# First attention of a two-layer transformer kernel: GpSimd makes the layernorm's mean and variance of batches 0 to 6 by trees of additions, in place of VectorE's statistics

## The reference, cut to what matters

```python
def _layernorm(x, axis=-1, eps=1e-05):
    m = jnp.mean(x, axis=axis, keepdims=True)
    v = jnp.var(x, axis=axis, keepdims=True)
    return (x - m) / jnp.sqrt(v + eps)

x = L0_attn_x                                        # [8, 512, 128]
x = _layernorm(x + _L0_attn_ref(x, L0_attn_W_qkv), axis=-1)   # this layernorm is changed
x = _layernorm(x + _L0_ffn_ref(x, ...), axis=-1)     # mixture of experts
x = _layernorm(x + _L1_attn_ref(x, ...), axis=-1)    # attention with sigmoid weights
x = _layernorm(x + _L1_ffn_ref(x, ...), axis=-1)

def _L0_attn_ref(x, W_qkv):                          # 16 heads of 8 columns
    q, k, v = jnp.split(x @ W_qkv, 3, axis=-1)
    scores = jnp.einsum('bhnd,bhmd->bhnm', heads(q), heads(k)) / jnp.sqrt(128.0)
    attn = jax.nn.softmax(scores, axis=-1)
    return jnp.einsum('bhnm,bhmd->bhnd', attn, heads(v))   # back to [8, 512, 128]
```

## Time and profile before

| | |
|---|---|
| median of three runs | 1043.27 us (1043.18 to 1043.75) |
| profiled execution, first to last instruction | 1041.4 us |
| mean granted TensorE clock in it | 0.996 of full speed |
| repeat of one batch in the first attention | 44.15 us |
| VectorE busy, share of the span | 834.0 us, 80% |
| GpSimd busy, share of the span | 475.6 us, 46% |

### The profile page before, as it was taken

The page is one execution under the profiler, slowest core; times in us unless marked ns, Lnnn a source line. Parts: engine busy times, 40 slices in busy tenths (PEclk is TensorE's granted clock), DMA queues, the critical chain, the costliest instruction groups (busy, mean ns, idle before and its releaser), DMA issues. The chain is left out here.

```text
span 1041.4 us, 20120 instructions
## 1 busy us (share of the span) xinstructions
PE 995.5 (96%) x5835; PEld 475.4 (46%) x5835; DVE 834.0 (80%) x1874; ACT 729.9 (70%) x939; POOL 475.6 (46%) x483
## 2 busy tenths in 40 slices
PE   8899999999999999999999999999999999999996
PEld 3222222222222235888888887873332333222485
DVE  6889999999999977787888789897666666643677
ACT  2078777787777786555555555568898888899754
POOL 0332514325053725676777677576442244220275
PEclk9999999999999999999999999999999999999998
DMA  6553222131321003344324323443512331230011
GB/s 198 153 186 119 76 76 89 44 117 46 96 78 52 3 2 101 102 128 145 101 91 156 121 90 117 137 137 102 172 65 61 121 119 63 60 122 1 1 31 52
DMA packets 73981, 97.04 MB, mean 93 GB/s; under 512 B 12669, under 2 KB 42237, under 8 KB 73533
## 3 DMA queue, kind: packets, MB, share of 16 engines
q1 hardware_dynamic: 73928, 96.40, 29.7%
HBM read 68.18 MB, written 27.79 MB: 92 GB/s over the span
## 5 line engine op out<-in xcount | busy, mean ns | idle before, releaser
L741 DVE TENSOR_REDUCE a_nmax<-a_ps_f 128x1 f32<-128x512 f32 x512 | 320.1, 683 | 20.2 <-PE a_ps_f L579 19.7
L497 ACT ACTIVATE a_prob<-a_ps_s 128x1024 f32<-128x1024 f32 x256 | 251.7, 1023 | 77.8 <-PE a_ps_s L646 76.5
L1367 ACT ACTIVATE a_prob<-a_ps_s 128x1024 f32<-128x1024 f32 x256 | 244.4, 1026 | 28.0 <-PE a_ps_s L1419 26.7
L2187 POOL TENSOR_TENSOR moe_hl<-moe_hid,moe_hh 128x512 fp32r<-128x512 f32 x134 | 173.9, 1303 | 84.3 <-ACT moe_hh L2068 84.2
L579 PE MATMUL a_ps_f<-a_ks,a_qs 48*128 48x512 bf16 x512 | 157.9, 386 | 11.8 <-DVE a_nmax L741 4.3
L2058 ACT ACTIVATE moe_ps<-moe_ps 128x512 f32<-128x512 f32 x128 | 74.5, 582 | 111.5 <-PE moe_ps L1981 110.7
L1432 PE MATMUL a_ps_o<-a_prob,a_va 128*32 128x512 f32 x1024 | 136.4, 605 | 1.4 <-DVE a_turned_o L1547 0.5
L659 PE MATMUL a_ps_o<-a_prob,a_va 128*32 128x512 f32 x1024 | 136.4, 605 | 0.5 <-ACT a_prob L497 0.4
L646 PE MATMUL a_ps_s<-a_qs,a_ks 51*128 51x512 bf16 x512 | 132.5, 381 | 1.7 <-ACT a_prob L497 1.5
L579 PEld LDWEIGHTS a_ps_f<-a_ks,a_qs 48*128 48x128 bf16 x512 | 39.7, 93 | 192.2 <-DVE a_nmax L741 162.2
L2109 DVE TENSOR_TENSOR moe_prod<-moe_cw,moe_ps 128x512 f32<-128x512 f32 x128 | 87.2, 681 | 27.4 <-PE moe_ps L1981 26.7
(11 more groups left out here) (302 smaller groups left out, 1640.1 us busy)
## 6 DMA issues: line engine op xcount, KB each, us to landing
moe_cw<-r_weights SPq DMA_DIRECT2D x256, 128.0 KB, 2.9
parts_q<-a_parts SPq DMA_DIRECT2D x48, 256.0 KB, 2.5
parts_k<-a_parts SPq DMA_DIRECT2D x48, 256.0 KB, 2.5
a_qs<-parts_q SPq DMA_DIRECT2D x126, 96.0 KB, 2.4
a_ks<-parts_k SPq DMA_DIRECT2D x126, 96.0 KB, 2.5
a_xt<-in_x_t SPq DMA_DIRECT2D x8, 256.0 KB, 2.8
out_x<-g_X SPq DMA_DIRECT2D x7, 256.0 KB, 2.3
moe_wg<-in_wg SPq DMA_DIRECT2D x1, 1088.0 KB, 6.6
```

What stands on the lines that cost most here:

```text
L497: nc.scalar.activation(prob[:, u % PSLOTS, :, :], ps_s[:, u % 2, :, :], ACT.Exp, scale=float(P) ** -0.5).then_inc(exp_done, 1)
L741: nc.vector.tensor_reduce(nmax[:, half_no, h % 2, col:col + 1], ps_f[:, bank, :], AX.X, ALU.max, negate=True).then_inc(max_done, 1)
L1367: nc.scalar.activation(prob[:, u % PSLOTS, :, :], ps_s[:, u % 2, :, :], ACT.Sigmoid, scale=float(HD) ** -0.5).then_inc(exp_done, 1)
L2187: nc.gpsimd.tensor_tensor(hl[:, part_at(j), :], hid[:, hid_at(j), :], hh[:, part_at(j), :], ALU.subtract).then_inc(hl_done, 1)
```

## The change

GpSimd now makes the mean and the variance of batches 0 to 6 itself. The function `stats` is gone from VectorE's program of the first attention. On GpSimd, `normalise(b)` runs where `layernorm_pool` and `layernorm_apply_pool` ran: it adds up the 128 columns of each row in seven halving additions (`sum_columns`), multiplies by 1/128 into the mean, subtracts the mean from `att`, squares, adds up the squares in seven more additions, multiplies by 1/128 into the variance, and goes on as before (epsilon, power, multiplication into X). Each step waits for the one before it. Three new buffers (`squares`, `half_sums`, `sums`), one of constants (`share`, one fill at the start) and one semaphore (`norm_step`) are added. Two counters that the later layernorm of batch 7 waits on are set forward once at the start of VectorE's program.

```diff
+LEVELS = 7
+NORM_STEPS = 2 * LEVELS + 4
...
+def sum_columns(pool, ops, src, half, to, step, at):
+
+    width = src.shape[2] // 2
+    ops.tensor_tensor(half[:, :, 0:width], src[:, :, 0:width], src[:, :, width:2 * width], ALU.add).then_inc(step, 1)
+    for k in range(1, LEVELS):
+        width //= 2
+        dst = half[:, :, 0:width] if width > 1 else to.unsqueeze(2)
+        pool.wait_ge(step, at + k)
+        ops.tensor_tensor(dst, half[:, :, 0:width], half[:, :, width:2 * width], ALU.add).then_inc(step, 1)
...
+            dve.sem_inc(ln["dve"], 2 * NT * (NB - 1))
+            dve.sem_inc(ln["centred"], NB - 1)
...
-            def stats(b):
-                dve.wait_ge(sum_done, b + 1)
-                layernorm_stats(nc, dve, ln, b, att)
-
...
-                            if tail and t == STATS_AT:
-                                stats(b - 1)
...
+            nc.gpsimd.memset(share[:, :], 1.0 / P)
...
+            def normalise(b):
+
+                at, spread, mean, var, rstd = NORM_STEPS * b, [P, NT, P], ln["mv"][:, :, 0], ln["mv"][:, :, 1], ln["rstd"]
+                pool.wait_ge(sum_done, b + 1)
+                sum_columns(pool, nc.gpsimd, att, half_sums, sums[:, :], norm_step, at)
+                pool.wait_ge(norm_step, at + LEVELS)
+                nc.gpsimd.tensor_tensor(mean, sums[:, :], share[:, :], ALU.mult).then_inc(norm_step, 1)
+                pool.wait_ge(norm_step, at + LEVELS + 1)
+                nc.gpsimd.tensor_tensor(att[:, :, :], att[:, :, :], ln["mv"][:, :, 0:1].broadcast_to(spread),
+                                        ALU.subtract).then_inc(norm_step, 1)
+                pool.wait_ge(norm_step, at + LEVELS + 2)
+                nc.gpsimd.tensor_tensor(squares[:, :, :], att[:, :, :], att[:, :, :], ALU.mult).then_inc(norm_step, 1)
+                pool.wait_ge(norm_step, at + LEVELS + 3)
+                sum_columns(pool, nc.gpsimd, squares, half_sums, sums[:, :], norm_step, at + LEVELS + 3)
+                pool.wait_ge(norm_step, at + 2 * LEVELS + 3)
+                nc.gpsimd.tensor_tensor(var, sums[:, :], share[:, :], ALU.mult).then_inc(norm_step, 1)
+                pool.wait_ge(norm_step, at + NORM_STEPS)
+                nc.gpsimd.tensor_tensor(ln["ve"][:, :], var, g["eps"][:, :], ALU.add).then_inc(ln["pool"], 1)
+                pool.wait_ge(ln["pool"], 2 * b + 1)
+                nc.gpsimd.tensor_tensor(rstd[:, :], ln["ve"][:, :], g["neg_half"][:, :], ALU.pow).then_inc(ln["pool"], 1)
+                pool.wait_ge(ln["pool"], 2 * b + 2)
+                nc.gpsimd.tensor_tensor(pool_gate[:, :], g["zero"][:, :], g["zero"][:, :], ALU.add)
+                nc.gpsimd.tensor_tensor(X[:, b, :, :], att[:, :, :], rstd[:, :].unsqueeze(2).broadcast_to(spread),
+                                        ALU.mult).then_inc(ln["x_done"], 1)
+
...
                     add_x(b - 1)
-                    layernorm_pool(nc, pool, g, ln, b - 1)
-                    layernorm_apply_pool(nc, pool, g, ln, b - 1, att, pool_gate)
+                    normalise(b - 1)
```

More of the change, by code:

```diff
@@ L332, in attention0 @@
         pool_gate = sb("pool_gate", [P, 1])
+        squares, half_sums, sums, share = sb("squares", [P, NT, P]), sb("half_sums", [P, NT, P // 2]), sb("sums", [P, NT]), sb(
+            "share", [P, NT])
         nmax = sb("nmax", [P, 2, 2, HH * NT // 2])
@@ L356, in attention0 @@
         s2_done, exp_done, pv_done = sem("s2_done"), sem("exp_done"), sem("pv_done")
-        o_taken, ot_done, rec_done, att_done, sum_done = (
-            sem(n) for n in ("o_taken", "ot_done", "rec_done", "att_done", "sum_done"))
+        o_taken, ot_done, rec_done, att_done, sum_done, norm_step = (
+            sem(n) for n in ("o_taken", "ot_done", "rec_done", "att_done", "sum_done", "norm_step"))
         S2_C, EXP_C, PV_C, O_C, OT_C, ATT_C = NU, 2, PSLOTS // 2, 1, 2, 1
```

## The result

The changed kernel takes 1045.49 us (median of 22 runs, 1044.84 to 1050.34), the kernel before in the same session 1043.74 us (22 runs, 1041.4 to 1047.12): ratio 1.0018, 95% interval 1.0011 to 1.0025. That is 1.75 us slower, near the edge of what can be told from no change, and 0.5 us above the top of the predicted range. The profiled execution spans 1043.3 us, against 1041.4 us.

A forecast was written before the change was run, and what follows sets the result against it. VectorE's maxima pace the first attention, but TensorE's own order and ScalarE's copy bound the place of the statistics. Profiled 1041.4 - 0.1 + 0 + 1.9 us around the span = 1043.2 us (84%), range 1041.5 to 1045.0 us.

The forecast's parts named there:

- The removal: First attention, VectorE: 1.19 us of statistics per batch hidden by the V product; gain 0 to 0.03 us in six batches.
- The chain: GpSimd's normalisation per batch: 12.77 us where it took 9.15 us, X ready 3.6 us later.
- Who waits for it: Splits of q, k and maxima queued behind GpSimd's chain: 1.2, 0.1 and 0.1 us late, slack 2.9 us, cost 0.
- The second rival: GpSimd's chain becomes the bound and TensorE waits for its splits: 1046.2 us, large case 1064 us; chance 7%.
- VectorE beside GpSimd: GpSimd's longer work doesn't slow VectorE's maxima (680 ns either way): price 0; only routing steps after 383 us could be blocked.
- the third rival: VectorE's maxima slowed by GpSimd beside them, ten more in each of six batches, 35 ns each: 1045.3 us; chance 2%.
- a few tenths, for things that I costed at nothing: Upper bound of the no-change case, for the whole kernel: a few tenths of a us for rounding and uncosted things.

The follow-up runs named there:

- the delayed kernel: Kernel before, plus one unread VectorE reduction of a 128x128 constant ahead of routing step 5 in the experts' loop repeats; 1044.77 us, ratio 1.0012.
- the kernel with the moved increment: Changed kernel with one one-time semaphore increment moved from VectorE's program to GpSimd's; 1044.36 us, ratio 1.0006 to the kernel before.

## Why the prediction was wrong

Forecast was no change; measured 1.75 us more than before, 1.2 us of it by one mechanism that I had priced at nothing.

**The removal: right.** I had followed TensorE through the V product to find that the statistics lie in its shade, with 0.9 to 1.0 us of new idle time ahead of maximum 16 and 0.2 us ahead of maximum 19. The trace has 0.93 and 0.19 us. Taking them out alone is worth 0 (0.9999), putting them back costs 0.

**The chain: right.** 12.77 us predicted, 12.59 us measured. The first tree takes 2.94 us with its gaps (195.26 to 198.20 us; 2.91 predicted from the slope between 32 and 512 columns). The squares are the whole difference: they take 1.04 us, and I had used the 1.27 us of an addition of two tensors. They differ from it in the operation and in that both inputs are one tensor; which of the two counts was not tested.

**Who waits for it: right.** q's split follows at once, 0.9 us late, k's waits 0.19 us for ScalarE, the maxima's split is on time to 0.01 us. The room I had worked out as 2.9 us measures 2.9 us. The second rival did not occur. Its price beyond the room was too low: I had 0.6 us for 0.6 us, and a repeat gets 3.64 us longer where the wait is 2.38 us, because TensorE's granted clock is 0.50 behind the wait.

**VectorE beside GpSimd: right for the maxima, wrong for what I left out.** The maxima take 683 ns on the mean in both kernels, so the third rival did not occur either. But here is the step that failed. Having weighed whether GpSimd's work holds VectorE's, I let it matter only for routing steps that the last chain could run on into. The routing steps and GpSimd's subtractions stand side by side in every repeat of the experts' loop, chain or no chain, and in the trace of before one of them ended 0.05 us ahead of GpSimd's start, while the same line in the last batch showed the price of missing that edge:

```profile
638.31 0.86 DVE L1801 COPY r_gneed<-r_top 128x16 f32<-128x16 f32 x1
```

The bound "a few tenths, for things that I costed at nothing" was too small by this 1.2 us: it ought to have been the largest jump that a small shift sets off somewhere else, here 1.2 us at one place, and 0.3 us in each of five repeats in the delayed kernel. What set it off, the pause of 0.20 us, no row of before could have shown.

The Trainium skill ("SBUF — State Buffer", section "🔬 SBUF: two separate sides") says of a GpSimd operation and a VectorE operation in a two-port mode, or with two inputs in SBUF, that whichever starts first gets the shared ports for its whole instruction, and the other blocks fully. The traces agree in one direction: each of the held copies and additions of the routing ends 0.02 to 0.04 us after a GpSimd operation, whatever its own size (0.14 to 0.18 us when free), and a copy that starts 0.03 us ahead of GpSimd's operation is not held. No trace shows which mode these operations ran in. In the other direction nothing shows: the subtraction that starts 0.03 us behind such a copy takes 1.29 us, as elsewhere. And one row doesn't fit "for its whole instruction": with five more operations the last chain does run on into the routing steps, as I had considered, and a copy that starts 0.06 us behind GpSimd's power takes 0.17 us.

```profile
407.84 0.17 DVE L1841 COPY r_gneed<-r_top 128x16 f32<-128x16 f32 x1
```

```profile
407.78 1.02 POOL L854 TENSOR_TENSOR a_rstd<-a_ve,g_neg_half 128x4 f32<-128x4 f32 x1
```

**The rest.** The start-up is 0.56 us longer in the profiled execution, and I had no term for it. It is also the part that varies most from kernel to kernel without a reason in their text (the second split of the maxima comes between 59.2 and 62.0 us), with TensorE's granted clock from 42 to 46 us at 0.57 before and 0.50 after. That it belongs to the change is not established: the kernel with the moved increment reaches the mark at 59.45 us, as before, and its runs are still 0.6 us over before, with an interval that includes none. A drift of 0.02 to 0.05 us in each of four repeats is unexplained as well.

## What to carry to other kernels

Where an engine's statistics lie in the shade of another engine's product, moving them to a third gains nothing, and following the product's own chain through the place, with the bank it needs, tells so before anything is built. A part that adds up to zero is not a kernel that stays the same, though: moving a single instruction can shift later work by tenths, and a place where a short VectorE copy ends just ahead of a GpSimd operation can turn such a tenth into a microsecond. Look for them in the trace of before (the same short operation at 0.14 us in one repeat and 0.86 us in another is the mark), put their price into the range, and use a form that runs beside GpSimd where one exists. A delay can free a held operation as well as hold a free one, so the price is read from a repeat's length and not from the one operation.

## What the runs showed of the hardware

- A copy of 128x16 float32 elements takes 0.14 to 0.17 us on VectorE when it starts ahead of GpSimd's addition or subtraction of 128x512, by as little as 0.03 us, and 0.85 to 1.23 us when it starts 0.1 to 0.5 us behind; a tensor_reduce with the same data takes 0.13 to 0.17 us either way. Behind GpSimd's power of 128x4 (1.02 us) the copy took 0.17 us, in the one row that there is. A tensor_scalar of 128x4 is held like the copy (1.00 us, 0.16 us free), with elements four or eight bytes apart; a reciprocal of the same elements is not (0.18 us).
- VectorE can pause for 0.20 us with nothing to wait for, at the first passage of a loop, depending on where the loop stands in its program: with the loop at instructions 644 and 645 it shows, at 643, 652, 660, 671 and 673 not.
- On GpSimd an addition of 128x4 takes 0.20 us, five from 128x128 down to 128x8 take 1.77 us with their gaps, 128x256 takes 0.73 us, and 128x512 takes 1.27 us from two tensors; the squares, a multiplication of 128x512 with both inputs the same, take 1.04 us.
- A wait of TensorE of 2.38 us was followed by some 3 us at a granted clock of 0.50 (1.2 GHz), which cost 1.26 us more, in each of five repeats.
